# Attention a: a 128x512 product without a reader for each pair of heads, the check of the flags between products and maxima, and three biases added by GpSimd

## What is computed

```python
topk = max(1, int(Tx * 0.3))                      # 76 of 256
scale = Dx ** (-0.5)
qkv = x @ W_qkv.T + b_qkv                         # 16 heads of 8
scores = einsum('bhid,bhjd->bhij', q, k) * scale
topk_scores, indices = jax.lax.top_k(scores, topk)
masked = full_like(scores, -inf).at[..., indices].set(topk_scores)
attn = softmax(masked, axis=-1)
out = einsum('bhij,bhjd->bhid', attn, v)          # heads side by side again
return out @ W_out.T + b_out
```

## Time and profile before

| | |
|---|---|
| median of 3 runs | 5267.58 us (5265.76 to 5270.42) |
| profiled execution | 5265.15 us, span 5263.4 us |
| granted TensorE clock, mean over the span | 0.825 |
| busy: PE, DVE, ACT, POOL | 4658.4, 4036.3, 3171.8, 2510.5 us |
| attention a | from some 50 us to some 2500 us of the span |
| one turn of its loop (four steps) | 147.1 us |

### The profile page before, as it was taken

The page is one execution under the profiler, slowest core; times in us unless marked ns, Lnnn a source line. Parts: engine busy times, 40 slices in busy tenths (PEclk is TensorE's granted clock), DMA queues, the critical chain, the costliest instruction groups (busy, mean ns, idle before and its releaser), DMA issues. The chain is left out here.

```text
span 5263.4 us, 121608 instructions
## 1 busy us (share of the span) xinstructions
PE 4658.4 (89%) x34686; PEld 3252.0 (62%) x34686; DVE 4036.3 (77%) x14232; ACT 3171.8 (60%) x10273; POOL 2510.5 (48%) x3026
## 2 busy tenths in 40 slices
PE   4588888888879888887899999899999998999998
PEld 3344444444444444443688888666666666888887
DVE  3899999999989999999588888655555555888886
ACT  3688888888868888887222222377776774222222
POOL 1466666666656666677444444311111112444444
PEclk6566666666666666666899999999999999999999
DMA  2000000000000000000334444100000001344444
GB/s 70 10 14 10 13 10 13 13 10 13 10 10 13 10 13 11 12 13 7 66 81 81 81 87 89 39 12 11 11 11 10 10 10 36 81 81 89 87 83 97
DMA packets 358576, 188.40 MB, mean 36 GB/s; under 512 B 190691, under 2 KB 346886, under 8 KB 358150
## 3 DMA queue, kind: packets, MB, share of 16 engines
q1 hardware_dynamic: 358150, 183.55, 17.3%
HBM read 147.04 MB, written 11.01 MB: 30 GB/s over the span
## 5 line engine op out<-in xcount | busy, mean ns | idle before, releaser
L854 ACT ACTIVATE junk<-SS,nt 128x256 bf16<-128x256 f32 x3072 | 1516.8, 502 | 141.8 <-POOL nt L482 96.8
L494 POOL TENSOR_SCALAR gone<-SS,mid 128x256 bf16<-128x256 f32 x1024 | 1184.7, 1172 | 628.3 <-DVEq L1041 483.4
L1204 POOL TENSOR_TENSOR f_hid<-f_g_m,f_cbs 128x256 f32<-128x256 f32 x1024 | 743.7, 726 | 852.8 <-DVE f_g_m L1449 656.9
L1304 ACT ACTIVATE f_th<-bank 128x256 f32<-128x256 f32 x1088 | 417.1, 383 | 1149.1 <-PE bank L1235 1149.1
L1234 PE MATMUL bank<-f_xTf,wgT 128*128 128x256 f32 x2176 | 692.8, 400 | 52.3 <-DVE f_g_m L1449 36.4
L1850 DVE TENSOR_REDUCE nmxb<-bank 128x2 f32<-128x512 f32 x512 | 329.6, 686 | 476.0 <-PE bank L1622 475.9
L1235 PE MATMUL bank<-f_xTf,wuT 128*128 128x256 f32 x2176 | 651.5, 381 | 0.0
L1266 PEld LDWEIGHTS bank<-wdT,f_hid 128*128 128x128 f32 x4096 | 601.6, 191 | 67.0 <-POOL f_hid L1204 12.7
L1266 PE MATMUL bank<-wdT,f_hid 128*128 128x128 f32 x4096 | 629.7, 276 | 10.5 <-POOL f_hid L1204 10.4
L854 ACT ACTIVATION_READ_ACCUMULATOR junk<-SS,nt 128x1 f32 x3072 | 597.0, 194 | 0.0
L644 PE MATMUL bank<-k,q 32*128 32x256 f32 x2048 | 422.8, 547 | 166.8 <-DVE SS L968 163.1
(11 more groups left out here) (232 smaller groups left out, 7849.0 us busy)
## 6 DMA issues: line engine op xcount, KB each, us to landing
f_cbs<-f_shares SPq DMA_DIRECT2D x512, 256.0 KB, 5.8
q4x<-q SPq DMA_DIRECT2D x64, 256.0 KB, 2.4
k4x<-k SPq DMA_DIRECT2D x64, 128.0 KB, 2.1
qrow<-q_rows SPq DMA_DIRECT2D x512, 8.0 KB
q_rows<-qTb SPq DMA_DIRECT2D x32, 128.0 KB, 1.7
out_dram<-xres SPq DMA_DIRECT2D x4, 1024.0 KB, 9.3
q4x<-max_rows SPq DMA_DIRECT2D x128, 4.0 KB
f_shares<-f_combT SPq DMA_DIRECT2D x64, 32.0 KB, 1.4
```

What stands on the lines that cost most here:

```text
L494: last = pool.tensor_scalar(gone[:, h % 4, i, :], SS[:, (u - lag) % 4, c, :], mid[:, (u - lag) % 4, 0, c:c + 1], 0.0, ALU.subtract, ALU.min)
L854: nc.scalar.activation(junk[:, c % 2, :], SS[:, uu % 4, c, :], ACT.Sign, bias=bias(c), accum_out=acc[:, k, uu % 4, c:c + 1]).then_inc(s["s ...
L1204: pool.tensor_tensor(hid[:, e % NBUF, :], g_m[:, e % NBUF, :], cbs[:, par, e, :], ALU.mult).then_inc(s["hid"], 1)
```

## The change

- Before the products of each pair of heads in the removal, TensorE multiplies `ident` with 512 columns of `wgT` into the bank `PT[a % 2]`, which the first `below_max` then writes anew. Nobody reads the result.
- `check_flags` moves from ahead of `largest` at h == 4 into it, behind the two products and ahead of the maxima.
- The three products with a row of ones go. `bv`, `bo` and `bq` are now loaded on all partitions, and GpSimd adds them: `bq` to `qtok` in odd steps behind the first move (semaphore `qrows`, awaited by `take_mom`), `bv` while it copies `vraw` to `vaug4`, `bo` to the rows of `xres` right after that (semaphore `biased`, awaited by VectorE before it adds the projection).

```diff
-                sp.dma_start(bv[:, :], b_qkv[2 * D:3 * D].rearrange("(a n) -> a n", a=1)).then_inc(s_w, 16)
-                sp.dma_start(bo[:, :], b_out.rearrange("(a n) -> a n", a=1)).then_inc(s_w, 16)
+                sp.dma_start(bv[:, :], b_qkv[2 * D:3 * D].rearrange("(a n) -> a n", a=1).to_broadcast([P, D])).then_inc(s_w, 16)
+                sp.dma_start(bo[:, :], b_out.rearrange("(a n) -> a n", a=1).to_broadcast([P, D])).then_inc(s_w, 16)
...
+                def biased_rows(n):
+
+                    wait(pool, s["m0c"], n + 1)
+                    pool.sem_inc(s["pgate"], 1)
+                    pool.tensor_tensor(qtok[:, :, :], qtok[:, :, :], bq[:, :].unsqueeze(1).to_broadcast([P, HALVES, D]), ALU.add).then_inc(s["qrows"], 1)
+
                 front(0)
+                pool.wait_ge(s["inid"], 32)
+                biased_rows(5)
                 guess(0, 0)
...
+                    if not even and ahead:
+                        biased_rows(m0_before(bb, "qtok"))
                     if runs(t, 2):
                         wait(pool, s["okay"], t - 1)
...
-                        pool.tensor_copy(vaug4[:, par, :, :, 0:HD].rearrange("p t h d -> p (t h) d"), vraw[:, :, :]).then_inc(s["vput"], 1)
+                        pool.tensor_tensor(vaug4[:, par, :, :, 0:HD],
+                                           vraw[:, :, :].rearrange("p (t h) d -> p t h d", t=HALVES),
+                                           bv[:, :].rearrange("p (h d) -> p h d", d=HD).unsqueeze(1).to_broadcast([P, HALVES, H, HD]),
+                                           ALU.add).then_inc(s["vput"], 1)
+                        wait(pool, s["xn"], bb + 1)
+                        pool.sem_inc(s["pgate"], 1)
+                        rows = xrow2(bb)
+                        pool.tensor_tensor(rows, rows, bo[:, :].unsqueeze(1).to_broadcast([P, HALVES, D]), ALU.add).then_inc(s["biased"], 1)
...
-                sp.dma_start(bq[:, :], b_qkv[0:D].rearrange("(a n) -> a n", a=1)).then_inc(s["inid"], 16)
+                sp.dma_start(bq[:, :], b_qkv[0:D].rearrange("(a n) -> a n", a=1).to_broadcast([P, D])).then_inc(s["inid"], 16)
...
-                        nc.tensor.matmul(M0[:, h * P:(h + 1) * P], xT[:, h * P:(h + 1) * P], wvT[:, :], start=True, stop=False)
-                        last = nc.tensor.matmul(M0[:, h * P:(h + 1) * P], ones1[:, :], bv[:, :], start=False, stop=True)
+                        last = nc.tensor.matmul(M0[:, h * P:(h + 1) * P], xT[:, h * P:(h + 1) * P], wvT[:, :], start=True, stop=True)
...
                             wait(pe, s["turned"], TURNED * (g + 1))
                             wait(pe, s["pt"], 8 * g + a)
+                            nc.tensor.matmul(PT[a % 2][:, :], ident[:, :], wgT[:, 0:4, :].rearrange("p k e -> p (k e)"), start=True, stop=True)
                             for k in range(2):
                                 below_max(v, a, k)
...
-                def take_mom(b, n, q):
+                def take_mom(b, n):
                     wait(dve, s["m0"], n + 1)
                     dve.sem_inc(s["gate"], 1)
-                    wait(dve, s["m0c"], q)
+                    wait(dve, s["qrows"], b + 1)
...
+                    def checked():
+                        if runs(t, 2):
+                            check_flags()
+                        yield
...
-                        if h == 4 and runs(t, 2):
-                            check_flags()
...
+                            dve.sem_inc(s["gate"], 1)
+                            wait(dve, s["biased"], bb - 1)
                             for i in range(HALVES):
                                 n = V.tensor_tensor(xrow(bb - 2, i), xrow(bb - 2, i), M1[:, i * P:(i + 1) * P], ALU.add)
...
-                            largest(1, h - 1, chosen if h <= 2 else iter(()))
+                            largest(1, h - 1, chosen if h <= 2 else checked() if h == 4 else iter(()))
```

More of the change, by code:

```diff
@@ L78, in build @@
         ident = sb("ident", [P, P])
-        ones1 = sb("ones1", [1, P])
         wqsT = sb("wqsT", [P, CH, P])
@@ L84, in build @@
         wvT = sb("wvT", [P, D])
-        bv = sb("bv", [1, D])
+        bv = sb("bv", [P, D])
         woT = sb("woT", [P, D])
-        bo = sb("bo", [1, D])
+        bo = sb("bo", [P, D])
         wqT = sb("wqT", [P, D])
@@ L198, in _ @@
                 pool.affine_select(out=mask_h16[:, :], in_=mask_h16[:, :], compare_op=ALU.is_ge, fill=0.0, base=0,
-                                   pattern=[[-HD, H]], channel_multiplier=1)
-                pool.memset(ones1[:, :], 1.0).then_inc(s_ones, 1)
+                                   pattern=[[-HD, H]], channel_multiplier=1).then_inc(s_ones, 1)
                 pool.wait_ge(s_ones, 2)
@@ L354, in build @@
         bnat = ab("bnat", [P, 1])
-        bq = ab("bq", [1, D])
+        bq = ab("bq", [P, D])
         ones128 = ab("ones128", [P, 1])
@@ L360, in build @@
         s = sems("a", "mv rstd xn m0 m0c m1 m1c var sig scores evac signs u0 u1 u2 thr failed flag okay "
-                      "copied turned spgate out pused pt pv on own aown pown slow oc gate pgate upper vput ini inid")
+                      "copied turned biased qrows spgate out pused pt pv on own aown pown slow oc gate pgate upper vput ini inid")
         max_rows = nc.dram_tensor("max_rows", (P, GT), f32, kind="Internal").ap()
@@ L483, in move, with xrow2 @@
                         pool.wait_ge(s[done], t + 1)
+                    def xrow2(b):
+                        if isinstance(b, int):
+                            return xres[:, b * HALVES:(b + 1) * HALVES, :]
+                        return xres[:, bass.ds(b * HALVES, HALVES), :]
                     def outsiders(lag, heads):
@@ L611, in q_rows @@
                     for h in range(HALVES):
-                        nc.tensor.matmul(M0[:, h * P:(h + 1) * P], xT[:, h * P:(h + 1) * P], wqT_a[:, :], start=True, stop=False)
-                        last = nc.tensor.matmul(M0[:, h * P:(h + 1) * P], ones1[:, :], bq[:, :], start=False, stop=True)
+                        last = nc.tensor.matmul(M0[:, h * P:(h + 1) * P], xT[:, h * P:(h + 1) * P], wqT_a[:, :], start=True, stop=True)
                     last.then_inc(s["m0"], 1)
@@ L715, in project_o @@
                         for i in range(HALVES):
-                            nc.tensor.matmul(M1[:, i * P:(i + 1) * P], oT[:, i * P:(i + 1) * P], woT[:, :], start=True, stop=False)
-                            last = nc.tensor.matmul(M1[:, i * P:(i + 1) * P], ones1[:, :], bo[:, :], start=False, stop=True)
+                            last = nc.tensor.matmul(M1[:, i * P:(i + 1) * P], oT[:, i * P:(i + 1) * P], woT[:, :], start=True, stop=True)
                         last.then_inc(s["m1"], 1)
@@ L946, in _ @@
                 take_g(1)
-                take_mom(0, 6, 6)
+                take_mom(0, 6)
                 own.end()
@@ L973, in largest @@
                         if not runs(t, lag):
+                            next(between, None)
                             return
@@ L1064, in step @@
                             if h == 5:
-                                take_mom(bb + 1, m0_before(bb, "mom"), m0_before(bb, "qtok") + 1)
+                                take_mom(bb + 1, m0_before(bb, "mom"))
                         if h == 7 and not even and tail:
                             wait(dve, s["m1"], m1_before(bb, "y") + 1)
+                            dve.sem_inc(s["gate"], 1)
+                            wait(dve, s["biased"], bb - 1)
                             for i in range(HALVES):
```

## The result

| | before | with the change |
|---|---|---|
| median | 5266.67 us (5262.15 to 5270.42, 4 runs) | **5338.93 us** (5336.75 to 5349.59, 4 runs) |
| ratio, 95% interval | | **1.0142** (1.0124 to 1.0159) |
| span, mean granted clock | 5263.4 us, 0.825 | 5334.9 us, 0.865 |

The kernel became 1.4% slower, where 2% faster was predicted. The time is 121 us over the range's upper end, 5218.

What follows compares the result with a forecast made beforehand. VectorE and TensorE were both taken as near their limit, TensorE at half speed most of the time. Terms: -68 - 47 - 4 + 13 = -106 us against the profiled 5265.15, giving 5159; range 5135 to 5218.

Steps and rivals of the forecast that it cites:

- Room to spare: TensorE in attention a: at full clock, 25.5 us of work in a step of 35, product included.
- With a faster TensorE that goes too.: Flags check in odd steps: the remaining 0.64 us of wait also vanishes, as TensorE no longer makes the flags late.
- The clock: TensorE in attention a: the added product lifts the granted clock from 0.66 to near 0.9.
- rival 1: Attention a: clock stays, TensorE becomes the bound, +170 us, 5435; below a granted 0.77 the kernel is slower; chance 0.12.
- The look, -68: VectorE's flags check, moved behind two products: 0.88 us of work covers its wait, -68 us, bounds -51 and -71.
- Waits for scores, -47: VectorE's waits for TensorE's scores: all go with TensorE at full clock, -47 us, bounds 0 and -47.
- GpSimd's chain, +13: GpSimd's chain from the check to `hi_t`: VectorE comes earlier and waits, 0.8 us a turn over 16 turns, +13 us.
- Biases, -4: Bias products leave TensorE for GpSimd: four go at the start, 2.9 us, two in the last projection, 1.4; -4 us.
- GpSimd's extra work is hidden: Bias additions on GpSimd: at most 2.2 us a batch, in its idle time or ahead of VectorE's need, costing nothing.
- The product's own length: Each unread 128x512 product on TensorE: 2.08 us at half clock, 1.1 at full.
- of the kind that goes before a rise: The unread product on TensorE: full-array work, like the full-array products seen ahead of a clock rise to 2.4 GHz.

Runs made afterwards that it cites:

- e9: The change with the unread product ahead of the second pair of heads only (64 of 256): 5387.92 us, ratio 1.0228.
- e7: The change with the product at all pairs of heads but the second (192 of 256 stay): 5238.38 us, ratio 0.9945.
- e6: The change, all four products kept, with the sum of failed rows moved ahead of the weighing: 5250.54 us, ratio 0.9968.
- e5: The change without the product, with the sum of failed rows moved ahead of the weighing: 5157.11 us, ratio 0.9794.
- e14: The change with the sum right behind the second pair's product and ScalarE's flag copy ahead of its exponentials at h == 4: 5242.18 us, ratio 0.9952.
- e15: The change without products, sum ahead of the second pair's block, flag copy ahead of the exponentials at h == 4: 5159.78 us, ratio 0.979.
- e3: The kernel before with only the look at the flags moved behind the two products: 5246.52 us, ratio 0.9955.
- e1: The change without the unread product; moved look and biases on GpSimd stay: 5197.39 us, ratio 0.9857.
- e8: The change with the product cut to 128 of 512 columns: 5237.90 us, ratio 0.9949.
- e10: The change with the product on only 32 of the array's columns, still 512 moving columns: 5374.03 us, ratio 1.0213.
- e11: The kernel before with the look moved and the sum of failed rows ahead of the weighing, no product: 5242.00 us, ratio 0.9955.

## Why the prediction was wrong

- **"Room to spare", the step that failed.** The product was weighed by throughput, 25.5 us of a step of 35, and so put at nothing on the path. By throughput that holds: at the clock that it got, TensorE works 31.8 us of a step of 38.0 in the change (417.9 of 500), against 32.1 of 36.8 before. But what others wait for inside a step has to be priced by its place, and there the products cost 142 us where nothing was put. The largest single part is the chain to the flags: TensorE's work between one eviction and the sum of the failures counts at its full length, and the product at the second pair lies in it with 2.08 us. That this place is the dear one is shown by e9 (191 us for it alone) against e7 (41 for the other three). But the flags aren't the whole. With the sum early the four still cost 93 us (e6 over e5), with the flags' chain cut as far as it goes 82 (e14 over e15). So some 60 of the 142 went over the flags, and 82 go over other waits for TensorE, whose paths were not cut. The chain stood in the rows read then: ScalarE's wait for the sum said that TensorE's order sets the flags' time; but what stands ahead of the sum had no term.
- **"With a faster TensorE that goes too."** The step took a higher mean clock for a higher clock at this place. There TensorE comes out of an idle stretch, mostly at 1.2 GHz, with the product (41 of 52) or without it (the scores at 1101.06, 2.08 us).
- **The clock.** It rose, as forecast, but to 0.77 (0.75 over 200 to 2300 us), not to 0.9. That is on the border that rival 1 named for holding the step. But in its account a slow kernel has TensorE short of time, and TensorE idles 6.2 us a step where it idled 4.6. So rival 1 had the side right and the mechanism wrong: the clock did not stay, and TensorE isn't the bound.
- **The look, -68.** In e3 it was worth 21 us. The products do cover the wait (55.4 to 22.7 us), but VectorE then comes early to `hi_t` and to the moments. **Waits for scores, -47:** 41.5 to 27.8 us in the change, some 14. **GpSimd's chain, +13:** the place was right; the wait for `hi_t` is 15.5 us in e1, and 27.3 with the product. **Biases, -4:** 7 alone. As terms of a sum they were the wrong idea: 7, 49 or 85 us, by what else sets the pace.
- Right: the clock rises and TensorE is busy less; GpSimd's extra work is hidden (VectorE waits 15.5 us for `hi_t` with it in e1, 16.8 without it in e3). The product's own length was right too: 2.08 and 1.13 us, where 2.08 and 1.1 were forecast. That e5 and e15 run at 5157 and 5160, close to the forecast 5159, is chance: they have no product and an earlier sum. The change without the product runs 5197.

What stays open is how the 82 us come about. ScalarE's longer wait for the removal (199.3 against 94.2 us) and VectorE's for scores and moments are where to look, but no run cuts one of these paths. The 11 us for each of the three other products are shown only as a difference.

## What to carry to other kernels

Before work is put on an engine with idle time, write down which engine waits for it in the same step, and what has to be made between that wait's start and its end: on that stretch each added microsecond counts at least in full (here 3.0 us for a product of 2.08), at the clock of that stretch, not at the mean. Off it the work wasn't free either: 11 us for a product in every step. A sum of small results that a branch waits for goes as early in the order as its inputs allow (here 40 us for three moved lines). When one wait is removed, price the others anew: the same bias products were worth 7 us and 85, and the moved look gained 21 or cost 14.

## What was unexpected of the hardware

- The granted clock doesn't follow added work alone, and what sets it these runs don't show. From 1000 to 1500 us it is 0.74 in e3, which adds nothing to TensorE, against 0.66 before; 0.62 with one product a step (e9), 0.77 with three (e7) or four; 0.72 with four of 128 columns (e8).
- The share of the array makes little difference here: 32 of 128 columns at work give 0.75 (e10), all of them 0.77. The reading that the new product is "of the kind that goes before a rise" because it fills the array has that against it.
- Being busy doesn't bring it: in e11 TensorE is busy 454.5 of 500 us, the most of all runs, at 0.63. In the change it works from 1052.68 to past 1064 us without a pause at half clock.
